# A mixture of experts computed for the two chosen experts of each token only, with rows scattered to per-expert tiles in DRAM

## The reference, cut to what matters

```
logits = xf @ Wr + br                                  # xf: layernormed tokens, 8 experts
topk_w, topk_idx = top_k(logits, 2)
topk_w = softmax(topk_w)
gate = sum(one_hot(topk_idx, 8) * topk_w[..., None], axis=1)
h = relu(einsum('th,ehf->etf', xf, W1) + b1[:, None, :])   # 128 -> 256
y = einsum('etf,efh->eth', h, W2) + b2[:, None, :]         # 256 -> 128
x = x + 0.5 * einsum('te,eth->th', gate, y)
```

## Time and profile before

| | |
|---|---|
| time, median of 3 runs | 1616.53 us (1612.32 to 1623.77) |
| profiled execution, its own time | 1617.13 us |
| its span | 1615.4 us |
| PE busy | 1412.7 us, 87% |
| DVE busy | 1005.8 us, 62% |
| ACT busy | 878.3 us, 54% |
| POOL busy | 424.8 us, 26% |
| DMA queue q1, share of 16 engines | 25.3% |

### The profile page before, as it was taken

One profiled execution on the slowest core, in us unless ns is written; L12 is line 12 of the kernel. 1 busy time (PEld: TensorE's weight loads), 2 busy tenths in 40 slices (PEclk: granted clock), 3 DMA queues, 4 the chain that ended last, 5 costly groups with the idle time before them and its releaser, 6 DMA issues. The chain is left out here.

```text
span 1615.4 us, 37203 instructions
## 1 busy us (share of the span) xinstructions
PE 1412.7 (87%) x11945; PEld 980.0 (61%) x11945; DVE 1005.8 (62%) x3167; ACT 878.3 (54%) x1559; POOL 424.8 (26%) x709
## 2 busy tenths in 40 slices
PE   2688888888769999997899969999799997999998
PEld 1466666666547777775555545555455555777776
DVE  2477887787636767676456555666566665545553
ACT  2466666666424434442577747777566664334343
POOL 4355565565310000111233322323222220000000
PEclk9799999999869999998799989999899998999999
DMA  5312222322100000000445543454344440000000
GB/s 130 79 51 70 78 51 66 78 60 68 32 2 1 11 11 10 11 15 23 121 122 135 126 115 94 116 133 120 87 117 121 103 118 23 8 8 13 6 6 13
DMA packets 62787, 102.97 MB, mean 64 GB/s; under 512 B 7942, under 2 KB 51934, under 8 KB 53470
## 3 DMA queue, kind: packets, MB, share of 16 engines
q1 hardware_dynamic: 62686, 101.76, 25.3%
HBM read 80.60 MB, written 20.97 MB: 63 GB/s over the span
## 5 line engine op out<-in xcount | busy, mean ns | idle before, releaser
L1126 ACT ACTIVATE e_buf<-ps_q 128x1024 f32<-128x1024 f32 x192 | 196.2, 1022 | 113.8 <-PE ps_q L1741 113.8
L1633 PEld LDWEIGHTS ps_o<-w,e_buf 128*128 128x128 f32 x2048 | 241.5, 192 | 23.1 <-issue 21.0
L1633 PE MATMUL ps_o<-w,e_buf 128*128 128x128 f32 x2048 | 250.6, 276 | 0.0
L2306 DVE SCALAR_TENSOR_TENSOR e_buf<-ps_o,gate,e_buf 128x128 f32<-128x128 f32 x512 | 144.0, 344 | 121.7 <-PE ps_o L1633 120.1
L1752 PE MATMUL ps_o<-e_buf,v_st 128*32 128x256 f32 x3072 | 208.8, 390 | 0.2
L1126 ACT ACTIVATE e_buf<-ps_k 128x1024 f32<-128x1024 f32 x192 | 195.5, 1018 | 13.8 <-PE ps_k L1741 12.0
L1062 ACT ACTIVATE e_buf<-ps_q,b_t 128x512 f32<-128x512 f32 x128 | 87.6, 686 | 147.7 <-PE ps_q L1625 145.9
L2047 DVE TENSOR_REDUCE mx<-ps_q 128x6 f32<-128x768 f32 x128 | 121.8, 952 | 64.8 <-PE ps_q L1340 63.8
L1062 ACT ACTIVATE e_buf<-ps_k,b_t 128x512 f32<-128x512 f32 x128 | 87.2, 687 | 131.7 <-PE ps_k L1625 130.0
L2520 DVE COPY o_sb<-ps_o 128x256 f32<-128x256 f32 x192 | 81.0, 422 | 107.8 <-PE ps_o L1752 64.8
L1741 PE MATMUL ps_q<-q_st,k_st 73*128 73x256 bf16 x768 | 121.4, 282 | 30.3 <-DMA q_st<-scr_q 18.2
(11 more groups left out here) (323 smaller groups left out, 2644.4 us busy)
## 6 DMA issues: line engine op xcount, KB each, us to landing
q_st<-scr_q SPq DMA_DIRECT2D x64, 576.0 KB
k_st<-scr_k SPq DMA_DIRECT2D x192, 192.0 KB
scr_q<-parts SPq DMA_DIRECT2D x64, 192.0 KB, 2.1
scr_k<-parts SPq DMA_DIRECT2D x96, 64.0 KB
out_dram<-x SPq DMA_DIRECT2D x8, 256.0 KB, 2.3
w<-in_L_ffn_W_dram SPq DMA_DIRECT2D x1, 1024.0 KB
e_buf<-in_L_attn_w_qkv_dram SPq DMA_DIRECT2D x1, 192.0 KB
k_st<-k_const SPq DMA_DIRECT2D x2, 56.0 KB
```

The costliest lines, as they stand in the source:

```text
L1126: act.activation(e_buf[g % 2][:, hp * 2 % HG:hp * 2 % HG + 2, :], (ps_q, ps_k)[hp % 2][:, :, :], ACT.Exp).then_inc(sem("fast_exp"), 1)
L1633: last = mm(ps_o[:, e % 2, t * P:(t + 1) * P], h_sb[e % 2][:, f, t * P:(t + 1) * P], w2[:, e * NF + f, :], start=f == 0, stop=f == NF - 1)
L2306: last = stt(acc[u][:, t, :], ps_o[:, e % 2, t * P:(t + 1) * P], gate[u][:, t, e:e + 1], acc[u][:, t, :], ALU.mult, ALU.add)
```

## The change

The mixture works on NC = 4 chunks of CB = 4 sequences (CT = 8 tiles, 1024 tokens), twice as large as a group. For a chunk the ranks of both groups give the two experts of each token. PE counts, with small bf16 products against a triangular matrix (`positions`), which place a token takes among those of its expert; DVE (`slots`, 15 steps) turns that into two row numbers for each token, into the expert of each of SLOTS = 2*8+7 = 23 tiles, and into two weights. POOL scatters the normed rows with 16 indirect DMAs (128 rows of 512 bytes each) into slots_in in DRAM (`send`). SP loads quads of 4 tiles. PE transposes a tile, multiplies it with W1 of the tile's expert (256 columns at once), transposes the result back after the relu, and multiplies it with W2; the biases are products of a row of ones with three bf16 parts of the bias, ahead of each. The expert's number is read from SBUF into a register on PE (`owner_of`), and the operands' addresses come from it. ACT does two copies of 128x256 for each tile, and two of up to 128x512 for each quad. SP stores the quad into slots_out, and when the chunk is done POOL gathers two rows for each token with 16 more indirect DMAs (`fetch`), and DVE adds them to x with their weights (`collect`). There are 92 tiles of 128 rows in a mixture, where there were 64 of 512.

The front of the next chunk stands between the tiles; `second_front` does that of the second group of chunk 0 ahead of each mixture. The keys of two groups stand behind the last tile of the chunk, and those of group NG - 2 behind everything. The rest of the diff renames and merges semaphores, and fills slots_in and the biases once ahead of the first mixture.

```diff
+CB = 4
+CT = CB * NT
+NC = B // CB
+SLOTS = 2 * CT + EXP - 1
+QUADS = (SLOTS + 3) // 4
+QT = 4
...
+def load_quad(m, q):
+    k = m * QUADS + q
+    if k >= 2:
+        sp.wait_ge(sem("X_t"), k - 1)
+    n = in_quad(q)
+    sp.dma_start(xs[:, k % 2, 0:n, :],
+                 slots_in[m % 2].rearrange("(i p) c -> p i c", p=P)[:, q * QT:q * QT + n, :])\
+      .then_inc(sem(f"tile_in_{k % 2}"), 16)
+def store_quad(m, q):
+    k = m * QUADS + q
+    n = in_quad(q)
+    sp.wait_ge(sem("E_yc"), k + 1)
+    sp.dma_start(slots_out[m % 2].rearrange("(i p) c -> p i c", p=P)[:, q * QT:q * QT + n, :],
+                 ys[:, k % 2, 0:n, :]).then_inc(sem(f"tile_out_{k % 2}"), 16)
+def chunk(m):
+    sp.wait_ge(sem(f"sent_{m % 2}"), (m // 2 + 1) * 2 * CT * 16)
+    load_quad(m, 0)
+    load_quad(m, 1)
+    for q in range(QUADS):
+        if q + 2 < QUADS:
+            load_quad(m, q + 2)
+        if m >= 2 and q == 0:
+            sp.wait_ge(sem("D_got"), (m - 1) * CT)
+        store_quad(m, q)
...
+sp.wait_ge(sem("D_slots"), 2)
+biases()
+for m in range(NC):
+    chunk(m)
+    if m:
+        key_parts(2 * m - 2)
+        key_parts(2 * m - 1)
+key_parts(NG - 2)
...
+def send(m):
+    pool.wait_ge(sem("D_slots"), m * 2 + 2)
+    if m == 0:
+        pool.wait_ge(sem("stored"), 80)
+    if m >= 2:
+        pool.wait_ge(sem("X_t"), (m - 1) * QUADS)
+    for t in range(CT):
+        for k in range(2):
+            pool.indirect_dma_start(
+                slots_in[m % 2], bass.IndirectOffsetOnAxis(ap=slot_no[m % 3][:, k, t:t + 1], axis=0),
+                normed_rows(m * 2 + t // GT)[:, t % GT, :], None).then_inc(sem(f"sent_{m % 2}"), 16)
+def fetch(m, w):
+    j = m * (CT // 2) + w
+    if w == 0:
+        for i in range(2):
+            pool.wait_ge(sem(f"tile_out_{i}"), (m + 1) * QUADS // 2 * 16)
+    if j >= 2:
+        pool.wait_ge(sem("D_got"), (j - 1) * 2)
+    for t in range(2 * w, 2 * w + 2):
+        for k in range(2):
+            pool.indirect_dma_start(
+                y_back[:, t % 4, k, :], None, slots_out[m % 2],
+                bass.IndirectOffsetOnAxis(ap=slot_no[m % 3][:, k, t:t + 1], axis=0))\
+                .then_inc(sem(f"back_{w % 2}"), 16)
+send(0)
+for m in range(NC):
+    for w in range(CT // 2):
+        if m:
+            fetch(m - 1, w)
+    if m + 1 < NC:
+        send(m + 1)
+    if m:
+        key_parts(2 * m - 2)
+        key_parts(2 * m - 1)
+for w in range(CT // 2):
+    fetch(NC - 1, w)
+key_parts(NG - 2)
...
+def positions(m):
+    pe.wait_ge(sem("D_sel"), m * 2 + 2)
+    w = CT * EXP
+    mm(ps_m[:, 0, 0:w], ahead_b[:, :], sel[:, :, :].rearrange("p t e -> p (t e)"), start=True, stop=False)
+    for t in range(CT - 1):
+        mm(ps_m[:, 0, (t + 1) * EXP:w], ones_b[:, 0:P],
+           sel[:, t, :].unsqueeze(1).broadcast_to([P, CT - 1 - t, EXP]), start=False, stop=t == CT - 2)
+    for t in range(CT):
+        last = mm(ps_m[:, 0, w:w + EXP], ones_b[:, 0:P], sel[:, t, :], start=t == 0, stop=t == CT - 1)
+    last.then_inc(sem("M_lg"), 1)
+def quad_tokens(m, q):
+    k = m * QUADS + q
+    pe.wait_ge(sem(f"tile_in_{k % 2}"), (k // 2 + 1) * 16)
+    if k:
+        pe.wait_ge(sem("X_tc"), k)
+    for t in range(in_quad(q)):
+        last = tr(ps_k[:, 1, t * P:(t + 1) * P], xs[:, k % 2, t, :])
+    last.then_inc(sem("X_t"), 1)
+def owner_of(m, i):
+    return pe.value_load(expert[m % 2][0:1, i:i + 1], min_val=0, max_val=EXP - 1)
+def hidden(m, i, e):
+    j, k, t = m * SLOTS + i, m * QUADS + i // QT, i % QT
+    to = tile_bank(j)[:, 0:HID]
+    if j >= 3:
+        pe.wait_ge(sem("E_htc"), j - 2)
+    mm(to, ones_b[0:3, 0:P], b1_rows[:, bass.ds(e, 1), :].rearrange("p e f -> p (e f)"), start=True, stop=False)
+    if t == 0:
+        pe.wait_ge(sem("X_tc"), k + 1)
+    mm(to, xt[:, k % 2, t * P:(t + 1) * P], w1[:, bass.ds(e, 1), :].rearrange("p e f -> p (e f)"),
+       start=False, stop=True).then_inc(sem("E_h"), 1)
+def hidden_t(m, i):
+    j = m * SLOTS + i
+    pe.wait_ge(sem("E_relu"), j + 1)
     for f in range(NF):
+        last = tr(tile_bank(j)[:, (NF + f) * P:(NF + f + 1) * P], h_sb[:, j % 4, f, :])
+    last.then_inc(sem("E_ht"), 1)
+def outputs(m, i, e):
+    j, k, t = m * SLOTS + i, m * QUADS + i // QT, i % QT
+    if t == 0 and k >= 2:
+        pe.wait_ge(sem("E_yc"), k - 1)
+    to = ps_o[:, k % 2, t * P:(t + 1) * P]
+    mm(to, ones_b[0:3, 0:P], b2_rows[:, bass.ds(e, 1), :].rearrange("p e c -> p (e c)"), start=True, stop=False)
+    pe.wait_ge(sem("E_htc"), j + 1)
+    for f in range(NF):
+        last = mm(to, ht[:, j % 4, f, :], w2[:, bass.ds(e * NF + f, 1), :].rearrange("p e c -> p (e c)"),
+                  start=False, stop=f == NF - 1)
+    if i % QT == in_quad(i // QT) - 1:
+        last.then_inc(sem("E_y"), 1)
...
+def chunk(m):
+    c = m % NC
+    ahead, keys = c + 1 < NC, m < NC and c > 0
+    ga = 2 * c - 2
+    pe.wait_ge(sem("D_slots"), m * 2 + 1)
+    if c == 0:
+        pe.wait_ge(sem("stored"), 112 + 32 * (m // NC))
+    quad_tokens(m, 0)
+    at = [owner_of(m, 0), owner_of(m, 1)]
+    hidden(m, 0, at[0])
+    hidden(m, 1, at[1])
+    hidden_t(m, 0)
+    for i in range(SLOTS):
+        if i % QT == 0 and i // QT + 1 < QUADS:
+            quad_tokens(m, i // QT + 1)
+        if i + 2 < SLOTS:
+            at.append(owner_of(m, i + 2))
+            hidden(m, i + 2, at[i + 2])
+        if i + 1 < SLOTS:
+            hidden_t(m, i + 1)
+        outputs(m, i, at[i])
+        if ahead:
+            if i == 1:
+                mix_tokens(2 * m + 2)
+            if i == 3:
+                mix_logits(2 * m + 2)
+            if i == 6:
+                mix_tokens(2 * m + 3)
+            if i == 8:
+                mix_logits(2 * m + 3)
+            if i == 12:
+                positions(m + 1)
+    if keys:
+        key_tokens(ga)
+        key_queries(ga)
+        key_keys(ga)
+        key_values(ga)
+        key_heads(ga)
+        key_tokens(ga + 1)
+        key_queries(ga + 1)
+        key_keys(ga + 1)
+        key_values(ga + 1)
+        key_heads(ga + 1)
...
+def slots(m):
...
+    dve.wait_ge(sem("M_lg"), m * 3 + 3)
+    dve.wait_ge(sem("M_lexp"), m * 2 + 2)
+    s(stt(square, ps_m[:, 0, w:w + EXP].unsqueeze(2).broadcast_to([P, EXP, EXP]), 1.0 / P, number,
+          ALU.mult, ALU.is_gt))
+    s(red(used[:, 0, :], square, AX.X, ALU.add))
+    s(tt(square, tri[:, :, :], used[:, 0, :].unsqueeze(1).broadcast_to([P, EXP, EXP]), ALU.mult))
+    s(red(used[:, 1, :], square, AX.X, ALU.add))
+    s(tt(used[:, 2, :], used[:, 0, :], used[:, 1, :], ALU.add))
+    s(stt(place, used[:, 1, :].unsqueeze(1).broadcast_to([P, CT, EXP]), float(P),
+          ps_m[:, 0, 0:w].rearrange("p (t e) -> p t e", t=CT), ALU.mult, ALU.add))
+    tt(ends, used[:, 2, :].unsqueeze(1).broadcast_to([P, SLOTS, EXP]),
+       tile_no[:, 0:SLOTS].unsqueeze(2).broadcast_to([P, SLOTS, EXP]), ALU.is_le)
+    for k in range(2):
+        last = stt(pick[:, k, :, :], rank[:, :, :], float(k), place, ALU.is_equal, ALU.mult)
+    s(last)
+    red(owner[:, :], ends, AX.X, ALU.add)
+    s(red(slot_f[:, :, :], pick, AX.X, ALU.add))
+    ts(expert[u][:, :], owner[:, :], float(EXP - 1), None, ALU.min).then_inc(sem("D_slots"), 1)
+    s(dve.tensor_copy(slot_no[m % 3][:, :, :], slot_f[:, :, :]))
+    dve.nop().then_inc(sem("D_slots"), 1)
+    s(stt(place, rank[:, :, :], 1.0, lexp[:, :, :], ALU.is_equal, ALU.mult))
+    s(red(weigh[:, 1, :], place, AX.X, ALU.add))
+    s(ts(weigh[:, 0, :], weigh[:, 1, :], 1.0, None, ALU.add))
+    s(dve.reciprocal(weigh[:, 0, :], weigh[:, 0, :]))
+    s(ts(gate[m % 3][:, 0, :], weigh[:, 0, :], 0.5, None, ALU.mult))
+    s(tt(gate[m % 3][:, 1, :], gate[m % 3][:, 0, :], weigh[:, 1, :], ALU.mult))
...
+def collect(m, w):
+    j = m * (CT // 2) + w
+    dve.wait_ge(sem(f"back_{w % 2}"), (j // 2 + 1) * 64)
+    for k in range(2):
+        for t in range(2 * w, 2 * w + 2):
+            xt_ = of_group(m % NC * 2 + t // GT)(t % GT)
+            last = stt(xt_, y_back[:, t % 4, k, :], gate[m % 3][:, k, t:t + 1], xt_, ALU.mult, ALU.add)
+        last.then_inc(sem("D_got"), 1)
+        dve.wait_ge(sem("D_got"), j * 2 + k + 1)
+    if w % 2:
+        dve.nop().then_inc(sem("M_x"), 1)
...
+def chunk(m):
+    c = m % NC
+    ahead, behind_, keys = c + 1 < NC, c > 0, m < NC and c > 0
+    ga = 2 * c - 2
+    if ahead:
+        g = c * 2 + 2
+        mix_stats(2 * m + 2, g)
+        dve.wait_ge(sem(f"sent_{m % 2}"), (m // 2 + 1) * 2 * CT * 16)
+        mix_norm(2 * m + 2, g)
+        mix_stats(2 * m + 3, g + 1)
+        mix_norm(2 * m + 3, g + 1)
+        mix_ranks(2 * m + 2)
+        mix_ranks(2 * m + 3)
+        slots(m + 1)
+    if behind_:
+        collect(m - 1, 0)
+        collect(m - 1, 1)
+    if keys:
+        key_stats1(ga)
+        key_norm1(ga)
+    if behind_:
+        collect(m - 1, 2)
+    if keys:
+        key_stats2(ga)
+    if behind_:
+        collect(m - 1, 3)
+    if keys:
+        key_norm2(ga)
+        key_stats1(ga + 1)
+        key_norm1(ga + 1)
+        key_queries(ga)
```

(53 more changed lines are left out.)

533 lines of the change are left out of this document (256 added, 277 removed).

## The result

The changed kernel takes 1855.2 us in the median of 4 runs (1839.35 to 1872.54), beside 1617.1 us for the kernel before (1612.32 to 1623.77): 1.137 times as long, with an interval of 1.130 to 1.144. The forecast was 1748 us, with a range of 1650 to 1860.

The account below looks back on a forecast made before the run. The prediction took PE, all but full in both mixtures, to bound the kernel before. It summed 1617 us, +91 for the first mixture and +40 for the second to 1748 us, range 1650 to 1860.

Parts of the forecast that it names:

- T = 1.75: PE's time for one mixture tile, bounded by its queue of load, addresses and pairs: 1.75 us, ends 1.4 and 2.4.
- two bf16 biases: PE's bias products in one tile, put at 0.16 us of its 1.37 us of work.
- PE alone would save some 80 us in each mixture: PE in each mixture: 23 tiles are 40 us for 1024 tokens, where two groups took 63.
- The quads' transposes: PE's transposes in a tile: three counted in its 1.21 us of work, at 0.11 us each.
- c = 1.15: POOL's price in us for one indirect DMA, scatter or gather; 136 stand in a row on the path.
- wait for `collect`: From chunk 1 on, POOL's last two gather windows wait for DVE: 1.7 + 8c more, 65.3 us from chunk to chunk.
- fills of slots_in: Fills beside the last causal rounds, costing some 15 us if that cover is gone.
- Two chains stand behind 23 tiles with nothing to cover them: First mixture's key chains behind a chunk's tiles: 27.2 us for two, within 87 us from chunk to chunk.
- Everything new is cheap: Rival for indirect DMAs and tiles: c = 0.4 and T = 1.4, 1596 us in all; chance 0.07.
- The pace of a landing: Rival for POOL's indirect DMAs: each goes at a landing's pace, c = 2.3, 1904 us in all; chance 0.08.
- The register load holds PE up: Rival for PE's tiles: load and addresses come on top of the work, T = 2.4, 1842 us; chance 0.14.
- A wash: Rival for the mixtures: c = 0.7, T = 1.55 and half of the keys' 27.2 us hidden, 1617 us; chance 0.06.

Follow-up runs that it names:

- e1: Changed kernel with each tile's expert a program constant, not read into a register (expert choice left out); 1839.8 us, ratio 1.141 to the kernel before.
- e5: Changed kernel without the tiles' two bf16 bias products, register loads kept; 1887.3 us, ratio 1.169 to the kernel before, on another chip.
- e2: Changed kernel with only each token's first expert: 8 scatters and 8 gathers for a chunk; 1751.9 us, ratio 1.082 to the kernel before.
- e3: Changed kernel with plain DMAs to and from fixed rows on POOL's queue instead of indirect ones (routing left out); ratio 1.083 to the kernel before.
- e4: Changed kernel plus unread products keeping PE busy in its waits for scatters; 1851.8 us, ratio 1.144 to the kernel before.
- e8: Changed kernel reordered: y_back holds eight tiles, next chunk's front ahead of first quad, key chains between tiles, later stores; 1999 us, ratio 1.230 to the kernel before.
- e9: Changed kernel without an edit, on another chip; 1959.5 us, ratio 1.214 to the kernel before.

## Why the prediction came out right, and 91 us short

The direction, the mechanism and the range held, and every stretch was longer than its term. Predicted and measured (from the windows above; the second mixture's wait counts from 1492.6), us:

| stretch | predicted | measured |
|---|---|---|
| wait ahead of chunk 0 | 38.5, 38.5 | 40.1, 38.6 |
| chunk 0 to 1 | 54.4, 54.4 | 63.5, 63.1 |
| first mixture, 1 to 2 and 2 to 3 | 87, 87 | 94.8, 98.4 |
| chunk 3 to the split of group 6 | 104.4 | 114.0 |
| second mixture, 1 to 2 and 2 to 3 | 65.3, 65.3 | 78.2, 78.5 |
| chunk 3 to the end | 69.7 | 86.7 |

- **PE for one tile, T = 1.75.** The size was near (1.86 at full clock), by two errors that cancelled. The step "I take T = 1.75 us, the queue as the bound" is wrong: e1 takes load and addresses away and the pace stays, e5 shows a tile pass in 1.10 us with them. The step before it is wrong too: "two bf16 biases, which I put at 0.16" cost 0.76. A bf16 product was priced from a row in which bf16 products follow each other; here each stands between f32 ones. 144 tiles x 0.11 = 16 us.
- **PE's saving.** "PE alone would save some 80 us in each mixture" came out as 9 and 30 us of busy time (the windows' sums above), by the same tiles of 1.86 us and more, and by the clock. The figure was loose from the start: 251 less 4 x 40 is 91, or 74 with the 4 us of front that the prediction gives each chunk later. The sum doesn't use it.
- **The quads' transposes.** The 1.21 us of a tile's work held the third transpose, but the pace taken for the sum was the queue's 1.75, which left no room for it: 0.44 us for each four tiles, 36 times, is 16 us more. The text had it in the work and lost it in the choice of the bound.
- **One indirect DMA, c = 1.15.** Measured 1.27; 136 x 0.12 = 16 us. The count of 136 is borne out by e2 (88 us for 68). The reason given was half right: a plain DMA of 128 rows is 0.54 (e3), and the row numbers add 0.73. The Trainium skill (DMA: Bandwidth & Descriptors, Latency and other measured facts) gives about 1 us for the emission of a DMA from GpSimd; the 0.97 us of work in an indirect one agrees, its distance of 1.27 and the plain one's 0.54 do not.
- **The clock.** The prediction expected it "below 0.99" and gave it no term. It is 0.50 in the waits and 0.72 to 0.88 in the chunks; at the lower level a tile takes 3.27 us. From a chunk's first tile to its last are 46.5 us in the fastest chunk with a front (1 of the first mixture) and 44.7 in the fastest without (3 of the first), and over these two values the other six have 18 us together (3.27 us tiles, and waits for quads' loads among them); e4 won 3 us a pause.
- **The rest,** 91 - 16 - 16 - 16 - 18 = 25 us, isn't assigned one by one. Part of it is the wait for `collect`: chunk 1 to 2 is 15.1 us longer than 0 to 1, and 10.9 were predicted, twice. The start of the mixtures was within 2 us, and the 15 us that the prediction feared from the fills of slots_in didn't come: PE's last product of the causal layers starts at 463.6 us, and at 465.9 before.
- **The keys.** "Two chains stand behind 23 tiles with nothing to cover them" is what the windows of 94.8 and 98.4 us show, 8 and 11 us over their 87. Whether an order that covers them is worth its 27 us stays open, since e8 ran only where copies of ACT were late.
- **Rivals.** *Everything new is cheap* falls with c = 1.27. *The pace of a landing* falls: landings take 2.5 us and overlap. *The register load holds PE up* falls by e1. *A wash* wanted half of the keys hidden; they weren't.

The chance of 0.88 for slower was right. The range held the profiled execution and the median near its upper end, and that it did was in part luck: on the chip of e9 the same kernel took 1959.5 us, 100 us above the range, with late copies of ACT that no term or rival of the prediction has. Where none were late it came out near the upper end because the terms erred to one side. The step that shows it best is the price of a bias: it was taken from a row in which such products follow each other, and here each stands between others of another kind.
